# A macaron transformer block on one core: the stores of the scaled attention outputs issued by GpSimd in place of SyncE

## The chip, the cores and the metric

The kernel runs on 1 core of one Trainium2 chip. The metric is the device time of one execution in microseconds (us). Of the kernel before, three runs are shown, and one more execution was taken with the hardware profiler.

## The reference, cut to what matters

The input is x, of 2 batches of 1024 rows and 1024 columns (f32). Three residual layers follow one another: half an FFN with a LoRA branch, an attention layer, and the same half FFN again.

```python
x = x + 0.5 * ffn(layernorm(x), ...)
x = x + attn(layernorm(x), ...)
x = x + 0.5 * ffn(layernorm(x), ...)
# attn, H = 32 heads, causal, latent keys and values of 64 columns
q = rmsnorm(x @ wq_a.T, q_a_ln_w) @ wq_b.T            # then rope on 64 of 128 columns
kv = rmsnorm(ckv, kv_a_ln_w) @ wkv_b.T
scores = einsum("bqhd,bkhd->bhqk", q_full, k_full) * softmax_scale
attn = softmax(where(causal, scores, min))
out = einsum("bhqk,bkhd->bqhd", attn, v).reshape(B, S, H * VD) @ wo.T
```

The division by the row sums of the softmax is put off: the kernel multiplies the product of probabilities and values by the reciprocal row sums afterwards. This multiplication and the store of its result are what the change is about.

## The kernel before, in words

`macaron_block` (L1320) runs six phases one after another: constants, the first FFN, latents, attention, output projection, the second FFN. Each phase is a block with one instruction stream per engine, and the streams are tied together by semaphores alone. In every phase all DMAs are issued by SyncE (SP); GpSimd (POOL) issues none.

**The attention phase** has 32 steps: 16 pairs of heads times 2 batches. A step handles 1024 queries of two heads. What an engine does in a step, and in which order, is written out by hand in one table per engine (L697 to L705). An entry such as `P0-1` is job P, number 0, belonging to the step before; `A0+1` belongs to the step after. `rounds` (L754) runs the tables: a first round, a loop over rounds of two steps, a last round. The jobs that matter here:

- PE: `Q` (L923) projects queries, `S` (L940) scores, `V` (L957) probabilities times values, `F` (L913) and `W` (L966) fold weights. After V of one step come S8, S9 of the next and then Q0, with F0 and F1 between them in every second step.
- ACT: `Q` copies the projected queries out of PSUM in three instructions (L1004 to L1006), `H` (L1013) makes their high part, `E` (L1021) are the exponentials, `O` (L1036) evicts half of the values.
- DVE: `M` (L1071) masks and takes maxima, `T` (L1081) transposes, `R` (L1090, L1094) prepares the reciprocal row sums, `O` (`join_values`, L1106) adds up the values into `o_raw`. Before it overwrites `o_raw` it waits for the store of the step before (`o_stored`).
- POOL: `A` (`rotate`, L1136, L1138, L1140) is rope on 64 partitions in three instructions, `B` (`query_lo`, L1145) the low part of the queries, `P` (`scale_values`, L1152) multiplies `o_raw` by `o_scale` and counts up the semaphore `scaled`. Before each job POOL waits until the job before has ended (`finished`, L1156). Its order in a step is B2 B3, A0 A1 B0 B1 of the next step, P0 P1 of the step before, A2 A3 of the next step.
- SP: `X` (`turn_scales`, L861, L865) brings the reciprocal row sums through DRAM into `o_scale`, `Y` (`store_o`, L871) waits for `scaled` and stores 128 x 512 f32 (256 KB) of `o_raw` to `oT`, `K` and `L` load weights, `Z` (L876) stores a folded weight. SP takes them strictly in the order of its table, so Y0 and Y1 stand in front of K, L, X0 and Z. After the rounds SP waits for the last stores (L895) before the block can end.

`o_raw` and `o_scale` are parts of the tile `pT`, and the trace names both by that.

The scores of rows from 512 on (S8 to S15) need the queries of B2 and B3: `scores` waits for `q_lo` (L932). A2 to B3 of POOL therefore stand between P1 and S8 of PE.

The output projection (`output_phase`) loads `oT` (L1209) and the folded weights (L1215) with SP as soon as the attention block has ended.

Of the kernel before, what the change touches and what calls it, by code (L numbers as in the profile page):

```python
# [16 lines left out]
P = 128  # L17
BANK = 512
B, S, D = 2, 1024, 1024
# [16 lines left out]
CHUNK = 512  # L36
# [43 lines left out]
def later(n, least):  # L80

    return not isinstance(n, int) or n >= least
# [619 lines left out]
            "T6+0 R0+0 T7+0 O0-1 M8+0 O1-1 F0+0 M9+0 O2-1 T8+0 F1+0 M10+0 M11+0 T9+0 O3-1 M12+0 M13+0 T10+0 T11+0 "  # L702
            "M14+0")
POOL_STEP = ("B2+0 B3+0 A0+1 A1+1 B0+1 B1+1 P0-1 P1-1 A2+1 A3+1")
SP_STEP = ("X1-1 Y0-1 Y1-1 K0+0 L0+0 X0+0 Z0+0")  # L705


def parse(table):
# [45 lines left out]
def rounds(eng, body):  # L754
    body(Round(0, first=True))
    with eng.Fori(1, PAIRS - 1) as it:
        body(Round(it))
    body(Round(PAIRS - 1, last=True))


def attention_phase(nc, k, args, oT_d, rinv_d, wvo_d, v_d):
# [6 lines left out]
    with ExitStack() as stack:  # L768
# [20 lines left out]
        valued, copied, evicted, scaled = c.sem("valued"), c.sem("copied"), c.sem("evicted"), c.sem("scaled")  # L789
        o_stored = [c.sem(f"o_stored{ch}") for ch in range(2)]  # L790
# [6 lines left out]
        def spare(e, t0, t1):  # L797

            return pT[:, e, t0:t1, CHUNK:S]

        qf, swapped = spare(0, 0, 2), spare(0, 2, 4)
        o_raw, o_scale = spare(1, 0, 2), spare(1, 2, 4)
# [19 lines left out]
        def folds(it, n, s):  # L822

            return 2 * (it + (s + 1) // 2) + n + 1
# [9 lines left out]
        @block.sync  # L834
        def _(sp):
            def load_fold(pair):
                sp.dma_start(wn[:], wn_d[bass.ds(pair, 1), :, :].rearrange("a p n -> (a p) n").rearrange("p (e n) -> p e n", e=2)).then_inc(wn_in, 16)
                sp.dma_start(wpe[:].rearrange("p e r n -> p (e r n)"), wpe_d[bass.ds(pair, 1), :, :].rearrange("a p n -> (a p) n")).then_inc(wn_in, 16)

            def load_out(pair):  # L840
                sp.dma_start(wv[:].rearrange("p e n -> p (e n)"), wv_d[bass.ds(pair, 1), :, :].rearrange("a p n -> (a p) n")).then_inc(wo_in, 16)
                sp.dma_start(wo[:].rearrange("p e n -> p (e n)"), wo_d[bass.ds(pair, 1), :, :].rearrange("a p n -> (a p) n")).then_inc(wo_in, 16)

            load_out(0)
            for j in range(2):
                sp.wait_ge(k.v_stored[j], 8 * NT)
            for b in range(B):
                for i in range(BLOCKS):
                    rows = v_d[b * S:(b + 1) * S, :].rearrange("(m a c) v -> c a m v", a=BLOCKS, c=32)
                    for a in range(BLOCKS):  # L850
                        sp.dma_start(val[32 * i:32 * i + 32, b, a, :, :], rows[:, a, :, :]).then_inc(v_in[b], 16)

            def turn_scales(it, ch, s):

                step, x = it * 2 + s, 2 * QT * (s % 2) + QT * ch
                rows = rinv_d[bass.ds(step, 1), ch * S:(ch + 1) * S].rearrange("a (c q) -> (a c) q", q=P)
                sp.wait_ge(r_turned, step * 2 + ch + 1)
                for g in range(BLOCKS):
                    if g == BLOCKS - 1 and later(step, 1):
                        sp.wait_ge(scaled, step * 2 + ch - 1)  # L860
                    sp.dma_start(rows[:, 32 * g:32 * g + 32], rinvT[32 * g + x:32 * g + x + QT, x // QT, :]).then_inc(r_stored, 16)  # L861
                sp.wait_ge(r_stored, step * 128 + ch * 64 + 64)
                for e in range(2):
                    x = ch * S + e * CHUNK
                    sp.dma_start(o_scale[KVR * e:KVR * e + KVR, ch, :],  # L865
                                 rinv_d[bass.ds(step, 1), x:x + CHUNK].to_broadcast([KVR, CHUNK])).then_inc(r_loaded[ch], 16)

            def store_o(it, ch, s):
                b, pair = s % 2, it + s // 2
                sp.wait_ge(scaled, (it * 2 + s) * 2 + ch + 1)  # L870
                sp.dma_start(oT_d[bass.ds(pair * P, P), b * S + ch * CHUNK:b * S + (ch + 1) * CHUNK], o_raw[:, ch, :]).then_inc(o_stored[ch], 16)  # L871

            def store_w(it, s):
                half, pair = s % 2, it + s // 2
                sp.wait_ge(w_copied, it * 2 + s + 1)
                sp.dma_start(wvo_d[bass.ds(pair * P, P), half * BANK:(half + 1) * BANK],  # L876
                             wvo[:]).then_inc(w_stored, 16)

            def body(r):
                for job, n, s in r.jobs(SP_STEP):  # L880
                    if job == "X":
                        turn_scales(r.it, n, s)
                    elif job == "Y":
                        store_o(r.it, n, s)
                    elif job == "Z":
                        store_w(r.it, s)
                    elif job == "L":
                        sp.wait_ge(f_split, folds(r.it, 1, s - 1))
                        load_fold(r.it + s // 2 + 1)
                    elif job == "K":  # L890
                        sp.wait_ge(w_copied, r.it * 2 + s + 1)
                        load_out(r.it + (s + 1) // 2)
            rounds(sp, body)
            for ch in range(2):
                sp.wait_ge(o_stored[ch], 16 * 2 * PAIRS)  # L895
            sp.wait_ge(w_stored, 16 * 2 * PAIRS)
# [231 lines left out]
        @block.gpsimd  # L1128
        def _(pool):
            def rotate(it, n, s):  # L1130

                ch, number = n // 2, (it * 2 + s) * 4 + n
                x = slice(ch * CHUNK, (ch + 1) * CHUNK)
                plain, crossed = qf[64:128, n % 2, :], swapped[64:128, n % 2, :]
                pool.wait_ge(q_copied, number + 1)
                nc.gpsimd.tensor_tensor(plain, plain, cosT[64:128, x], ALU.mult).then_inc(rope_parts, 1)  # L1136
                pool.wait_ge(rope_parts, number * 2 + 1)
                nc.gpsimd.tensor_tensor(crossed, crossed, sinT[64:128, x], ALU.mult).then_inc(rope_parts, 1)  # L1138
                pool.wait_ge(rope_parts, number * 2 + 2)
                nc.gpsimd.tensor_tensor(plain, plain, crossed, ALU.add).then_inc(roped, 1)  # L1140

            def query_lo(it, n, s):
                x = slice(n // 2 * CHUNK, (n // 2 + 1) * CHUNK)
                pool.wait_ge(q_hi, (it * 2 + s) * 4 + n + 1)
                nc.gpsimd.tensor_tensor(q[:, n % 2, LO, x], qf[:, n % 2, :], q[:, n % 2, HI, x].bitcast(F32), ALU.subtract).then_inc(q_lo, 1)  # L1145

            def scale_values(it, ch, s):

                step = it * 2 + s
                pool.wait_ge(evicted, step * 4 + 4)  # L1150
                pool.wait_ge(r_loaded[ch], step * 32 + 32)
                nc.gpsimd.tensor_tensor(o_raw[:, ch, :], o_raw[:, ch, :], o_scale[:, ch, :], ALU.mult).then_inc(scaled, 1)  # L1152

            pool.wait_ge(tab_in, 48)

            def finished(it, job, n, s):  # L1156
                if job == "P":
                    pool.wait_ge(scaled, (it * 2 + s) * 2 + n + 1)
                else:
                    pool.wait_ge(roped if job == "A" else q_lo, (it * 2 + s) * 4 + n + 1)  # L1160

            def body(r):
                job, n, s = list(Round(0).jobs(POOL_STEP))[-1]
                before = None if r.first else (job, n, s - 2)
                for job, n, s in r.jobs(POOL_STEP):
                    if before:
                        finished(r.it, *before)
                    before = job, n, s
                    if job == "A":
                        rotate(r.it, n, s)  # L1170
                    elif job == "B":
                        query_lo(r.it, n, s)
                    elif job == "P":
                        scale_values(r.it, n, s)
            rounds(pool, body)
# [246 lines left out]
```

## Time and profile before

| | us |
|---|---|
| median of 3 runs | 1962.72 |
| lowest and highest | 1962.16, 1965.12 |
| the profiled execution, own time | 1964.07 |
| its span, first to last instruction | 1962.1 |
| granted TensorE clock, mean | 0.974 of full |

Busy time in the span: PE 1819.1 (93%), the weight loads of PE 1423.7, DVE 1230.6, ACT 997.6, POOL 870.1 (44%). The profiled execution is 1.35 us above the median. Its own time is 1.97 us above its span. Where a row says `x2` after two instructions that follow one another closely, its duration is that of both together. `[4.62 <-ACT pT L1006]` behind a row says that the engine stood idle for 4.62 us before it and what released it.

### The profile page before, as it was taken

What the parts mean: (1) busy time and instruction counts of PE and PEld (TensorE: products, weight loads), DVE (VectorE), ACT (ScalarE), POOL (GpSimd) and SP (SyncE); (2) the same over time, 40 slices, a digit from 0 to 9 for tenths busy, and PEclk for the clock granted to TensorE, in tenths of its full rate; (3) what the DMA queues carried; (4) which work ended last, traced back from release to release, by engine and by line L of the source; (5) the groups of instructions that cost most, each with busy time, mean ns of one, the idle gap of its engine ahead of it and who ended that gap; (6) DMA issues with size and microseconds to landing.
All of it is one profiled execution on the core that took longest, in us unless ns stands there. A gap on an engine that the chain in (4) does not pass through costs nothing. (4 is left out here: it accounts for less than half of the span.)

```text
span 1962.1 us, 44377 instructions
## 1 busy us (share of the span) xinstructions
PE 1819.1 (93%) x15472; PEld 1423.7 (73%) x15472; DVE 1230.6 (63%) x2653; ACT 997.6 (51%) x2135; POOL 870.1 (44%) x641
## 2 busy tenths in 40 slices
PE   6999968689999999999999999997699999979999
PEld 4678767667777777777777777775488888857887
DVE  5555356378889889888898888887421121125553
ACT  2211055478888888888887888885410010012110
POOL 2231110268777787787877877873000000004311
PEclk9999989899999999999999999999799999989999
DMA  6442152402221221211212212211742223224321
GB/s 224 167 167 91 60 150 71 107 23 70 65 77 50 71 77 55 83 60 55 83 60 72 66 49 83 66 67 56 261 134 88 86 96 117 65 107 158 132 86 65
DMA packets 111695, 182.45 MB, mean 93 GB/s; under 512 B 27472, under 2 KB 64464, under 8 KB 109584
## 3 DMA queue, kind: packets, MB, share of 16 engines
q1 hardware_dynamic: 111632, 181.61, 28.5%
q8 instruction: 39, 0.64, 0.1%
q14 instruction: 24, 0.20, 0.0%
HBM read 122.06 MB, written 59.51 MB: 93 GB/s over the span
## 5 line engine op out<-in xcount | busy, mean ns | idle before, releaser
L940 PE MATMUL psS<-keyT,q 128*128 128x512 f32 (+2 forms) x2304 | 474.3, 351 | 32.7 <-POOL q L1145 25.3
L940 PEld LDWEIGHTS psS<-keyT,q 128*128 128x128 f32 x2304 | 381.9, 190 | 127.6 <-DVE negmax L1071 41.4
L1021 ACT ACTIVATE prob<-prob,negmax 128x640 f32<-128x640 f32 (+7 forms) x512 | 391.9, 767 | 78.7 <-DVE negmax L1071 76.4
L1081 DVE STREAM_TRANSPOSE pT<-prob 128x640 f32<-128x640 f32 (+7 forms) x512 | 380.2, 762 | 66.3 <-PE psV L957 63.3
L1071 DVE CUSTOM_DVE_ANT_0 prob<-psS,mask 128x640 f32<-128x640 f32 (+7 forms) x512 | 371.9, 742 | 40.0 <-PE psS L940 26.3
L413 PE MATMUL f_psy<-f_weff,f_xT 128*128 128x512 f32 x1344 | 313.9, 393 | 0.0
L1307 PE MATMUL o_psy<-o_w,o_o 128*128 128x512 f32 x1344 | 304.8, 389 | 0.0
L1136 POOL TENSOR_TENSOR pT<-pT,cosT 64x512 f32<-64x512 f32 x128 | 164.6, 1286 | 302.6 <-ACT pT L1006 288.5
L1307 PEld LDWEIGHTS o_psy<-o_w,o_o 128*128 128x128 f32 x1344 | 252.3, 188 | 52.3
L413 PEld LDWEIGHTS f_psy<-f_weff,f_xT 128*128 128x128 f32 x1344 | 250.8, 188 | 54.0 <-issue 1.7
L957 PE MATMUL psV<-pT,val 32*64 32x512 f32 (+3 forms) x8192 | 264.8, 407 | 6.6 <-DVE pT L1081 6.2
L957 PEld LDWEIGHTS psV<-pT,val 32*64 32x64 f32 x8192 | 168.0, 132 | 110.7 <-issue 67.4
L245 POOL TENSOR_TENSOR f_weff<-f_w_in,f_weff 128x1024 fp32r<-128x1024 f32 x16 | 38.7, 2416 | 450.9 <-ACT f_weff L341 450.9
L923 PE MATMUL psV<-qnT,wq 128*128 128x512 f32 x768 | 195.4, 398 | 0.4 <-DVE wq L1062 0.4
L1281 DVE TENSOR_TENSOR o_y<-o_psy,o_x_in 128x512 f32<-128x512 f32 x32 | 22.0, 692 | 261.0 <-PE o_psy L1307 246.3
L312 POOL TENSOR_TENSOR f_xo<-f_xt,f_bias_half 128x1024 f32<-128x1024 f32 x32 | 80.4, 2512 | 219.6 <-DMA out<-f_xo 101.1
L1145 POOL TENSOR_TENSOR q<-pT,q 128x512 fp32r<-128x512 f32 x128 | 165.2, 1290 | 11.5 <-POOL pT L1140 2.2
L1240 ACT ACTIVATE o_o<-o_in 128x1024 fp32r<-128x1024 f32 x32 | 32.5, 1053 | 269.9 <-PE o_psy L1307 234.7
L1138 POOL TENSOR_TENSOR pT<-pT,sinT 64x512 f32<-64x512 f32 x128 | 165.1, 1290 | 10.1
L1140 POOL TENSOR_TENSOR pT<-pT 64x512 f32<-64x512 f32 x128 | 164.6, 1286 | 10.0
L923 PEld LDWEIGHTS psV<-qnT,wq 128*128 128x128 f32 x768 | 142.1, 191 | 28.6 <-DVE wq L1062 0.6
L163 ACT ACTIVATE f_xT<-f_ps_xT 128x512 fp32r<-128x512 f32 x64 | 34.9, 595 | 178.7 <-PE f_ps_xT L154 178.7
(99 smaller groups left out, 1882.3 us busy)
## 6 DMA issues: line engine op xcount, KB each, us to landing
wo<-in_wo SPq DMA_DIRECT2D x16, 1024.0 KB, 5.6
pT<-row_scales SPq DMA_DIRECT2D x128, 128.0 KB, 2.8
oT<-pT SPq DMA_DIRECT2D x64, 256.0 KB, 2.4
o_in<-oT SPq DMA_DIRECT2D x32, 512.0 KB, 5.2
f_xt<-in_x SPq DMA_DIRECT2D x16, 512.0 KB, 4.1
f_w_in<-in_w SPq DMA_DIRECT2D x16, 512.0 KB, 6.9
w_sum<-f_w_in SPq DMA_DIRECT2D x16, 512.0 KB, 5.1
x<-f_xo SPq DMA_DIRECT2D x16, 512.0 KB, 3.0
```

Of the source, the lines that this page charges most:

```text
L413: ins = nc.tensor.matmul(psy[:, j, half, :], f.xT[:, j, a, dt, :], weff[:, b, m, dt, half * BANK:(half + 1) * BANK], start=(i == 0 and dt ...
L923: ins = nc.tensor.matmul(psV[:, n, :], wq[:, a, e, t, :], k.qnT[:, m, t, b * S + ch * CHUNK:b * S + (ch + 1) * CHUNK], start=(i == 0 and t ...
L940: ins = nc.tensor.matmul(psS[:, slot, start + x0:start + x1], q[:, e, a, t * P:(t + 1) * P], k.keyT[:, m, b * S + x0:b * S + x1], start=(i ...
L957: ins = nc.tensor.matmul(out[:, :, kt:QT, :], val[rows, b, block, kt, :], pT[rows, :, kt:QT, x:x + 32], start=(kt == 0 and a == 0), stop=( ...
L1021: nc.scalar.activation(row, row, ACT.Exp, bias=negmax[:, n % 8:n % 8 + 1], scale=-1.0, accum_out=rowsum[:, column(n, s):column(n, s) + 1]) ...
L1071: nc.vector.tensor_tensor_reduce(out=prob[:, n % RING, 0:width], in0=place(n), in1=k.mask[:, S - width:S], scale=-1.0, scalar=LARGEST, op0 ...
L1081: nc.vector.transpose(pT[:, n % 2, t, 0:width], prob[:, n % RING, 0:width]).then_inc(turned, 1)
L1136: nc.gpsimd.tensor_tensor(plain, plain, cosT[64:128, x], ALU.mult).then_inc(rope_parts, 1)
L1138: nc.gpsimd.tensor_tensor(crossed, crossed, sinT[64:128, x], ALU.mult).then_inc(rope_parts, 1)
L1140: nc.gpsimd.tensor_tensor(plain, plain, crossed, ALU.add).then_inc(roped, 1)
L1145: nc.gpsimd.tensor_tensor(q[:, n % 2, LO, x], qf[:, n % 2, :], q[:, n % 2, HI, x].bitcast(F32), ALU.subtract).then_inc(q_lo, 1)
L1307: ins = nc.tensor.matmul(psy[:, j, half, :], o[:, j, a, pair, :], w[:, m, pair, half * BANK:(half + 1) * BANK], start=(pair == 0 and i == ...
```

## The change

SP no longer stores `o_raw`. In its place POOL, right behind each multiplication of `scale_values`, waits until that has ended and issues the same DMA itself, with the same semaphore for its completion. The order of the other jobs is unchanged.

```diff
-SP_STEP = ("X1-1 Y0-1 Y1-1 K0+0 L0+0 X0+0 Z0+0")
+SP_STEP = ("X1-1 K0+0 L0+0 X0+0 Z0+0")
...
-            def store_o(it, ch, s):
-                b, pair = s % 2, it + s // 2
-                sp.wait_ge(scaled, (it * 2 + s) * 2 + ch + 1)
-                sp.dma_start(oT_d[bass.ds(pair * P, P), b * S + ch * CHUNK:b * S + (ch + 1) * CHUNK], o_raw[:, ch, :]).then_inc(o_stored[ch], 16)
...
-                    elif job == "Y":
-                        store_o(r.it, n, s)
...
                 nc.gpsimd.tensor_tensor(o_raw[:, ch, :], o_raw[:, ch, :], o_scale[:, ch, :], ALU.mult).then_inc(scaled, 1)
+                b, pair = s % 2, it + s // 2
+                pool.wait_ge(scaled, step * 2 + ch + 1)
+                nc.gpsimd.dma_start(oT_d[bass.ds(pair * P, P), b * S + ch * CHUNK:b * S + (ch + 1) * CHUNK], o_raw[:, ch, :]).then_inc(o_stored[ch], 16)
```

## Rows read from the trace of the kernel before

**Rows 1.** Two steps: length, busy PE, PEld, DVE, ACT, POOL, PEclk, DMA share, GB/s.

```profile
554.05:614.51 60.46, 58.94 (x720) 44.10 (x721) 52.85 (x124) 50.17 (x111) 46.37 (x36) 1.00 0.20 67
```

**Rows 2.** Timeline of POOL, one step: start, us, line, what, idle before.

```profile
825.62 2.65 POOL L1145 TENSOR_TENSOR q<-pT,q 128x512 fp32r<-128x512 f32 x2 [0.16 <-POOL pT L1140]
832.90 1.30 POOL L1136 TENSOR_TENSOR pT<-pT,cosT 64x512 f32<-64x512 f32 x1 [4.62 <-ACT pT L1006]
...
844.15 2.66 POOL L1152 TENSOR_TENSOR pT<-pT 128x512 f32<-128x512 f32 x2 [0.26 <-POOL q L1145]
...
855.21 2.64 POOL L1145 TENSOR_TENSOR q<-pT,q 128x512 fp32r<-128x512 f32 x2
```

**Rows 3.** Timeline of PE: S8 and S9 behind V; first, two neighbouring and last.

```profile
493.54 1.13 PE L940 MATMUL psS<-keyT,q 128*128 128x384 f32 x6 [0.28 <-POOL q L1145]
...
827.05 1.11 PE L940 MATMUL psS<-keyT,q 128*128 128x384 f32 x6 [0.36 <-POOL q L1145]
828.42 1.11 PE L940 MATMUL psS<-keyT,q 128*128 128x384 f32 x6 [0.26 <-POOL q L1145]
829.37 1.53 PE L923 MATMUL psV<-qnT,wq 128*128 128x512 f32 x6
...
856.54 1.16 PE L940 MATMUL psS<-keyT,q 128*128 128x384 f32 x6 [0.35 <-POOL q L1145]
857.91 0.65 PE L913 MATMUL psV<-wn 64*128 64x64 f32 x4 [0.21 <-DVE pT L1106]
...
1310.97 1.11 PE L940 MATMUL psS<-keyT,q 128*128 128x384 f32 x6 [0.17 <-POOL q L1145]
```

**Rows 4.** Timeline of ACT: the copy of Q0 out of PSUM.

```profile
831.01 0.60 ACT L1004 ACTIVATE pT<-psV 128x512 f32<-128x512 f32 x1 [0.76 <-PE psV L923]
```

**Rows 5.** Waits, 451 to 1328 us: who waited for whom, us, times, longest.

```profile
POOL pT L1136 <- ACT pT L1006: 153.3, 29, 6.2
...
PE psS L940 <- POOL q L1145: 13.3, 42, 0.4
...
POOL pT L1152 <- POOL q L1145: 6.0, 28, 0.3
```

**Rows 6.** Waits of SP's queue, whole run.

```profile
SPq L871 <- POOL pT L1152: 540.3, 64, 21.8
```

**Rows 7.** Instructions on oT: count, duration ns min/median/max, first and last start.

```profile
L871 SPq DMA_DIRECT2D oT<-pT x64: 348/362/373, 452.7 to 1376.6; - x64
```

**Rows 8.** DMA issues: out<-in, count, KB each, median us to landing.

```profile
oT<-pT SPq DMA_DIRECT2D x64, 256.0 KB, 2.4
```

**Rows 9.** Timelines at the first and last of the 30 affected steps.

```profile
462.42 2.63 POOL L1145 TENSOR_TENSOR q<-pT,q 128x512 fp32r<-128x512 f32 x2 [0.16 <-POOL pT L1140]
...
464.17 2.15 PE L940 MATMUL psS<-keyT,q 128*128 128x384 f32 x12
...
1338.72 2.64 POOL L1145 TENSOR_TENSOR q<-pT,q 128x512 fp32r<-128x512 f32 x2
...
1340.32 2.31 PE L940 MATMUL psS<-keyT,q 128*128 128x384 f32 x12
```

**Rows 10.** Timeline at the end of the attention phase.

```profile
1373.97 2.60 POOL L1152 TENSOR_TENSOR pT<-pT 128x512 f32<-128x512 f32 x2 [21.86 <-DVE pT L1106]
1375.26 1.70 SPq L871 DMA_DIRECT2D oT<-pT  x2
1379.51 1.02 SPq L1209 DMA_DIRECT2D o_in<-oT  x2
```

**Rows 11.** Start of the output projection: a PE pause, then stretches (columns of rows 1).

```profile
1400.11 39.97 PE L1295 MATMUL o_psy<-o_w,o_o 128*128 128x512 f32 x168 [2.87 <-DVE o_w L1267]
...
1400.00:1402.00 2.00, 1.89 (x6) 1.55 (x7) 2.00 (x2) 2.00 (x3) 0.00 (x0) 0.68 0.70 182
1402.00:1404.00 2.00, 2.00 (x7) 1.51 (x6) 2.00 (x3) 0.90 (x2) 0.00 (x0) 0.50 0.68 215
1404.00:1406.00 2.00, 2.00 (x10) 1.65 (x9) 1.73 (x2) 0.66 (x1) 0.00 (x0) 0.97 0.96 322
```

## The prediction, made before the changed kernel ran

> **What bounds the kernel now.** I read the stretches first. In the attention phase two steps take 60.46 us, in which PE is busy 58.94, DVE 52.85, ACT 50.17 and POOL 46.37 [rows 1]. PE looks like the bound and POOL like an engine with 14 us to spare. The waits say otherwise: between 451 and 1328 us PE waits for the low part of the queries 42 times, 13.3 us in all, while POOL's own idle time ends with a copy by ACT, 29 times, 153.3 us [rows 5]. Those two waits belong to one loop, which the timelines show.
>
> Take POOL from its idle time on: A0 starts at 832.90; A0 A1 B0 B1, then P0 P1 at 844.15, then A2 A3, then B2 at 855.21 [rows 2]. B2 is the first half of a 2.64 us pair, so it ends at 855.21 + 1.3 = 856.5, and PE's S8 starts at 856.54, released by it [rows 3]. The way back stands one step earlier: B3 ends at 825.62 + 2.65 = 828.27 [rows 2]; S9 starts at 828.42 and Q0 follows at 829.37 for 1.53 us [rows 3]; ACT begins to copy Q0 at 831.01, three instructions of 0.6 us [rows 4], to 832.8; A0 starts at 832.90 [rows 2]. No link has slack: POOL to PE to ACT to POOL. The 4.62 us (5.97 in every other step) that POOL stands idle are the time that PE and ACT need for their part of the loop, not room for more work. Whatever is put between A0 and B2 lengthens the step by its full time. S8 waits for POOL like this in 28 steps on end, from 493.54 to 1310.97 us [rows 3].
>
> **What is removed.** SP issues 64 stores at 0.36 us each [rows 7], 23 us of its queue, and stands 540.3 us in front of them waiting for POOL [rows 6]. This frees K, L and X0, which stand behind Y1 in SP's table, up to 20 us earlier. I cost the gain at nothing: in the steady stretch what POOL's P0 waits for is POOL itself [rows 5], not the row scales that SP brings, and no wait of PE is for a weight load. The scales of X0 still can't land before P0 of the step before has read the old ones.
>
> **What is added.** Two DMA issues on POOL per step, each behind its P. Each wait for `scaled` is for a multiplication whose end POOL waits for before its next job anyway; I cost the waits at nothing beyond the issue. Queued behind DMA 0 is P1; behind DMA 1 are A2, A3, B2, B3, and for B2 waits S8 of PE. So both issues lie in the loop.
>
> The price c of one issue on POOL is not in the trace, since no DMA is issued there. From below it is bounded by SP's issue of the same DMA, 0.36 us [rows 7]. From above I take POOL's own period for a whole 128 x 512 multiplication: P0 and P1 together take 2.66 and one takes 1.30, so 1.36 us [rows 2]. I take 1.0, nearer the upper end: what POOL does it does as an instruction of its own kind, with a hand-over of 0.16 us in front of it where it had to wait [rows 2], and a list of 128 rows is to be made. The Trainium skill (DMA: Bandwidth & Descriptors, "Latency and other measured facts") states about 1 us until the first byte of a DMA of GpSimd against 0.6 from SP, the difference being descriptors written by its own cores; if all of that 1 us held POOL, an estimate by that page would be the same sum as mine.
>
> **The sum**, against the profiled execution (1964.07 us, 1.35 above the median of the runs):
> - 30 steps have P0 and P1 ahead of A2 (those of steps 0 to 29; the last two P pairs come after the last B): 30 x 2 x 1.0 = +60.0.
> - Cover: in the first of them B2 ends at 462.42 + 1.31 = 463.73 and S8 starts at 464.17, so 0.44 is free; in the last 1338.72 + 1.32 = 1340.04 against 1340.32, 0.28 [rows 9]. In every other step F0 waits 0.21 for DVE behind S8 [rows 3]; 14 x 0.21 = 2.9. Together -3.6.
> - The end of the phase is on the path: the block closes when the last store has landed. DMA 0 delays P1 by 1.0, and the last store is given out 1.0 instead of 0.36 after P1's end. +1.6. The transfer itself, 2.4 us to landing [rows 8], is unchanged. Today the multiplications end at 1376.57 and the next load is issued at 1379.51 [rows 10].
> - DVE waits for the store before it overwrites `o_raw`. The store would land some 2.6 us later than today, and DVE has a whole step before it needs the tile: `o_stored` of a step is asked for behind the next step's V, which ends just before S8, some 9 us after P1 (844.15 + 2.66 = 846.81 to 856.54 [rows 2, 3]), against 2.6 + 2.4 us [rows 8]. Nothing.
> - POOL's P31 pair has 21.86 us of idle time before it [rows 10], so P30 costs nothing.
>
> 60.0 - 3.6 + 1.6 = +58.0. That is 2022.1 for the profiled execution and 1962.72 + 58.0 = 2020.7 against the median; I forecast 2020. With c = 0.36: 21.6 - 3.6 + 0.4 = +18.4, so 1981. With c = 1.36: 81.6 - 3.6 + 2.4 = +80.4, so 2043.
>
> **Rivals.**
> *The second issue is hidden.* P uses 128 partitions, A only 64 (the other half of the tile), yet both take 1.30 us [rows 2]: time follows the length, so half of POOL idles in A. If the part of POOL that makes the DMA isn't needed by A2, DMA 1 runs beside it, and only DMA 0 and a hand-over of about 0.1 are left: 30 x 1.1 = 33.0, - 3.6 + 1.6 = +31.0, 1993.7. The Trainium skill (GPSIMD Engine Reference, "2.1 Instruction dispatch") has this rule: each of POOL's cores goes on to the next instruction when its own share is done. Against it stands that nothing here shows two POOL instructions side by side; in this trace POOL waits for the end of each. Chance 0.17.
>
> *The clock falls.* The longer step shows as a PE pause before S8: 0.35 + 2c, plus 0.25 before S9. In the output projection a PE pause of 2.87 us was followed by a fall of the granted clock from 1.00 to 0.50, and PE ran 13 matmuls in 4 us where it runs 10 in 2 us at full clock: 7 fewer at 0.2 us, 1.4 us lost [rows 11]. With c = 1.0 the pause is 2.35 and stays under that. From c = 1.26 on it is as long. Then c = 1.3 gives 78.0 - 3.6 + 2.2 = +76.6, and with a fall in every third step 10 x 1.4 = +14 more: 2053; in every step +42, 2081. For it speaks that S8, S9 and Q0, which the fall would hit, are links of the loop. Chance 0.08.
>
> *Not slower.* If POOL only hands the transfer over, as SP's engine does in 0.36 us with others waiting for nothing, and spends far less than that, the two hand-overs vanish in the 3.6 us of cover. It decides from c below 0.13 us on: 60c - 3.6 + 2c - 0.36 is then under 3.9 us, which is 0.2% and about what a measurement of this kernel can tell from no change. At c = 0.05 it is -0.9 us: 1962. A true gain would need someone who waits for what SP can now issue earlier, and I found nobody. Chance 0.10, of it 0.02 for faster.
>
> *The issue costs POOL more than one of its multiplications* (c above 1.36, clock unchanged): each 0.1 adds 6.2 us. Chance 0.05.
>
> **Numbers.** The forecast, both issues paid, c between 0.36 and 1.36, has 0.60, and its own range is 1981 to 2043. The hidden second issue (0.17) lies inside it. To have 8 in 10 I take the upper end to 2055, which holds the fall of the clock in every third step and c up to 1.55. Left out are the not-slower case and the two upper tails. Slower by over 0.2%: 0.90; within: 0.08; faster: 0.02.
>
> **What would show it.** 64 DMA issues on POOL, none of `oT` on SP; two steps of 60.46 us grown to about 64.3; POOL's idle time before A0 unchanged at 4.6 and 6.0 us, since it is the other engines' part of the loop; PE's wait for POOL before S8 grown from 0.35 to about 2.35; between P0 and P1, and between P1 and A2, gaps of about 1 us each (a gap only before P1: the hidden issue); the granted clock still 1.00; SP's 540 us wait moved to other lines. I am wrong if the idle time before A0 shrinks by what the issues take: then it was slack after all. I am wrong in the price if the gaps are far from 1.0, and each 0.1 us of it is worth 6 us.

## The result and the profile after

The changed kernel takes 2081.86 us (median of 4 runs, 2079.43 to 2084.94) against 1962.65 for the kernel before: a ratio of 1.060, 95% interval 1.059 to 1.062. It is slower, as forecast, but by 119 us in place of 58, and outside the range (1981 to 2055). The span of the profiled execution grew from 1962.1 to 2081.7 us, by 119.6.

From the page of the changed kernel: busy time by engine; two DMA queues (packets, MB, share of 16 engines); the group that grew most (busy, mean ns, idle before it and its releaser); the moved DMA (KB each, us to landing).

```profile
PE 1871.4 (90%) x15472; PEld 1473.0 (71%) x15472; DVE 1232.3 (59%) x2653; ACT 992.8 (48%) x2135; POOL 906.7 (44%) x705
...
q1 hardware_dynamic: 102416, 164.83, 24.5%
q0 software_dynamic: 5120, 16.78, 2.1%
...
L933 PE MATMUL psS<-keyT,q 128*128 128x512 f32 (+2 forms) x2304 | 499.2, 366 | 97.9 <-POOL q L1138 89.1
...
oT<-pT POOLq DMA_DIRECT2D x64, 256.0 KB, 3.2
```

The 64 stores have left SP's queue for a software queue, and POOL has 641 + 64 = 705 instructions. PE's wait for POOL in front of the scores has become 89.1 us of idle time (25.3 in the kernel before). PE itself is busy 52 us longer (1871.4 against 1819.1) with the same 15472 matmuls: that is no wait, that is a slower clock.

POOL's timeline in the changed kernel, one step, to be laid beside [rows 2] (L1129 opens A, L1145 is P, L1148 the store, L1138 is B):

```profile
815.08 1.29 POOL L1129 TENSOR_TENSOR pT<-pT,cosT 64x512 f32<-64x512 f32 x1 [5.66 <-ACT pT L999]
...
826.33 1.29 POOL L1145 TENSOR_TENSOR pT<-pT 128x512 f32<-128x512 f32 x1 [0.26 <-POOL q L1138]
828.31 0.58 POOL L1148 DMA_DIRECT2D oT<-pT  x1 [0.69 <-POOL pT L1145]
828.91 1.31 POOL L1145 TENSOR_TENSOR pT<-pT 128x512 f32<-128x512 f32 x1
830.87 0.58 POOL L1148 DMA_DIRECT2D oT<-pT  x1 [0.65 <-POOL pT L1145]
831.53 1.27 POOL L1129 TENSOR_TENSOR pT<-pT,cosT 64x512 f32<-64x512 f32 x1
...
839.81 2.63 POOL L1138 TENSOR_TENSOR q<-pT,q 128x512 fp32r<-128x512 f32 x2
851.11 1.30 POOL L1129 TENSOR_TENSOR pT<-pT,cosT 64x512 f32<-64x512 f32 x1 [8.67 <-ACT pT L999]
```

An issue costs POOL 0.58 us and, ahead of it, 0.65 to 0.69 us in which it does nothing that is recorded: from P0 to P1 there are 2.58 us where there were 1.36, so 1.22 per issue. From A0 to the end of B3 there are 839.81 + 2.63 - 815.08 = 27.36 us, where it was 855.21 + 2.64 - 832.90 = 24.95 [rows 2]: 2.41 more per step. And the idle time in front of A0, which I had expected unchanged, is 8.67 us in one step (5.97 before) and 5.66 in the other (4.62 before). So something in the part of the loop that belongs to PE and ACT has become longer too. PE's timeline and the stretches of the same step show it (the stretches have the columns of [rows 1]):

```profile
841.13 1.15 PE L933 MATMUL psS<-keyT,q 128*128 128x384 f32 x6 [2.76 <-POOL q L1138]
...
843.25 1.97 PE L933 MATMUL psS<-keyT,q 128*128 128x384 f32 x6
...
846.19 2.93 PE L916 MATMUL psV<-qnT,wq 128*128 128x512 f32 x6
...
840.00:842.00 2.00, 0.87 (x6) 0.87 (x6) 0.83 (x2) 2.00 (x5) 1.92 (x2) 1.00 0.00 0
842.00:844.00 2.00, 2.00 (x9) 1.75 (x8) 1.49 (x4) 0.80 (x3) 0.44 (x1) 0.56 0.00 0
...
846.00:848.00 2.00, 2.00 (x6) 1.56 (x6) 1.32 (x5) 1.28 (x4) 0.00 (x0) 0.50 0.00 0
```

A PE pause of 2.76 us before S8; then the granted clock falls from 1.00 to 0.50, from 2.4 to 1.2 GHz, and S9 takes 1.97 us in place of 1.1, Q0 2.93 in place of 1.53. Read in short stretches over the attention phase, the clock falls behind 24 of the 30 lengthened pauses and stays down for 3 to 7 us each time, 130 us in all; in the same steps of the kernel before (451 to 1340 us) it never falls. The falls hit the very matmuls through which the loop runs.

**The theory** after this: two terms. 30 steps x 2.41 us of POOL, 72 us; and some 42 us from the clock. **Rivals:** (A) the issues and their software queue cost all of it, and the clock is a bystander that changes nothing, since PE waits for POOL anyway; (B) SP's new order brings data late.

### The profile page after: what moved, and what is told of

It reads as the page before. It is cut to its first block and busy times, and to the rows that moved or that the text cites. A ratio compares the mean times of both kernels' runs of the same rounds, so it can differ in the third digit from the quotient of the medians.

```text
span 2081.7 us, 44365 instructions
## 1 busy us (share of the span) xinstructions
PE 1871.4 (90%) x15472; PEld 1473.0 (71%) x15472; DVE 1232.3 (59%) x2653; ACT 992.8 (48%) x2135; POOL 906.7 (44%) x705
## 5 line engine op out<-in xcount | busy, mean ns | idle before, releaser
L933 PE MATMUL psS<-keyT,q 128*128 128x512 f32 (+2 forms) x2304 | 499.2, 366 | 97.9 <-POOL q L1138 89.1
L933 PEld LDWEIGHTS psS<-keyT,q 128*128 128x128 f32 x2304 | 409.0, 203 | 192.8 <-issue 50.7
L1129 POOL TENSOR_TENSOR pT<-pT,cosT 64x512 f32<-64x512 f32 x128 | 164.2, 1283 | 346.5 <-ACT pT L999 333.5
L916 PE MATMUL psV<-qnT,wq 128*128 128x512 f32 x768 | 214.5, 426 | 0.4 <-DVE wq L1055 0.4
L916 PEld LDWEIGHTS psV<-qnT,wq 128*128 128x128 f32 x768 | 154.6, 208 | 32.5 <-DVE wq L1055 0.6
L1138 POOL TENSOR_TENSOR q<-pT,q 128x512 fp32r<-128x512 f32 x128 | 164.7, 1287 | 11.4 <-POOL pT L1133 2.2
L1006 ACT ACTIVATE q<-pT 128x512 fp32r<-128x512 f32 x128 | 80.2, 627 | 84.9 <-POOL pT L1133 82.4
```

The source lines that it names most:

```text
L916: ins = nc.tensor.matmul(psV[:, n, :], wq[:, a, e, t, :], k.qnT[:, m, t, b * S + ch * CHUNK:b * S + (ch + 1) * CHUNK], start=(i == 0 and t ...
L933: ins = nc.tensor.matmul(psS[:, slot, start + x0:start + x1], q[:, e, a, t * P:(t + 1) * P], k.keyT[:, m, b * S + x0:b * S + x1], start=(i ...
```

## Experiments: is it the clock, the issue or SP?

**One: keep PE busy in the pause.** The changed kernel, with extra matmuls in front of S8:

```diff
+                if n == 8:
+                    for _ in range(12):
+                        nc.tensor.matmul(psS[:, 0, P:BANK], k.keyT[:, HI, b * S:b * S + P], k.keyT[:, HI, b * S:b * S + BANK - P],
+                                         start=True, stop=True)
                 if t % 4 == 0:
                     pe.wait_ge(q_lo, step * 4 + t // 4 * 2 + e + 1)
```

> The changed kernel with 12 more matmuls of 384 columns on PE ahead of S8 in every step (they write the place in PSUM that S8 is about to fill; the result is not touched), some 2.2 us of work in a PE pause of 2.3 to 2.8 us. Theory (two terms: 1.22 us of POOL per issue in the loop, and a fall of the clock that the longer pause brings): the clock stays at 1.00 in the attention phase, POOL's idle time before A0 goes back to 4.6 and 6.0 us, and the time falls from 2082 to about 1963 + 30 x 2.44 - 3.6 + 2 = 2035 (2030 to 2045). Rival A (the whole loss is the issue on POOL and what comes with it, the clock is a bystander): the clock comes back and the time stays at 2075 or above. Rival B (SP's new order makes data late): no change either.

Measured: 2043.53 us, ratio 1.039 (1.036 to 1.042). 384 added matmuls (12 in each of 32 steps) make the kernel 42 us faster than the changed one (1.060 - 1.039 = 0.021 of 1964). Timelines of this kernel, PE, then POOL:

```profile
825.99 2.35 PE L926 MATMUL psS<-keyT 128*128 128x384 f32 x12 [0.15 <-issue]
828.65 1.16 PE L937 MATMUL psS<-keyT,q 128*128 128x384 f32 x6 [0.32 <-POOL q L1142]
...
802.54 1.30 POOL L1133 TENSOR_TENSOR pT<-pT,cosT 64x512 f32<-64x512 f32 x1 [4.65 <-ACT pT L1003]
...
835.92 1.29 POOL L1133 TENSOR_TENSOR pT<-pT,cosT 64x512 f32<-64x512 f32 x1 [5.96 <-ACT pT L1003]
```

The extra work lies in what was the pause, S8 follows at full clock, no fall is left in these steps, and POOL's idle times are those of the kernel before to 0.03 us. Rival A falls for these 42 us. Two steps now take 65.28 us (731.30 to 796.58) against 60.46: 2 x 2.41, the POOL term alone.

**Two: the same time on POOL without any DMA.** The kernel before, with a second, shorter multiplication per scaling. The first 432 of 512 columns of `o_raw` are scaled twice.

```diff
+                nc.gpsimd.tensor_tensor(o_raw[:, ch, 0:432], o_raw[:, ch, 0:432], o_scale[:, ch, 0:432], ALU.mult).then_inc(dummied, 1)
+                pool.wait_ge(dummied, step * 2 + ch + 1)
                 nc.gpsimd.tensor_tensor(o_raw[:, ch, :], o_raw[:, ch, :], o_scale[:, ch, :], ALU.mult).then_inc(scaled, 1)
```

> The kernel before, all stores by SP, with a second multiplication of 128 x 432 ahead of each scaling on POOL, some 1.1 us and a hand-over of 0.14: about the time of an issue. (The first 432 columns of o_raw are scaled twice.) No DMA is issued by POOL. Theory (it is only time on POOL, wherever it comes from): as the changed kernel, 2070 to 2090, with the same falls of the clock. Rival A in the form that the software queue itself costs (descriptors, transfers, contention): clearly less, 2035 or under. Rival B (SP's order): back to 1963 to 2035, since SP's order is the old one.

Measured: 2084.07 us, ratio 1.060 (1.054 to 1.066), with 21 falls of the clock and 119 us of half clock in the same steps. Its POOL timeline:

```profile
825.37 1.12 POOL L1153 TENSOR_TENSOR pT<-pT 128x432 f32<-128x432 f32 x1 [0.26 <-POOL q L1146]
826.57 1.29 POOL L1155 TENSOR_TENSOR pT<-pT 128x512 f32<-128x512 f32 x1
827.94 1.13 POOL L1153 TENSOR_TENSOR pT<-pT 128x432 f32<-128x432 f32 x1
829.15 1.28 POOL L1155 TENSOR_TENSOR pT<-pT 128x512 f32<-128x512 f32 x1
```

With SP's old order, with the old queue for every store and with 1.2 us of arithmetic per store, the loss is the same within the intervals, which are some 12 us wide to either side. The two terms need neither the software queue nor SP's new order: rival B falls. It is time on POOL in this place. What an interval of 12 us would hide is the few us that POOL's own stores cost at the end of the phase; they are read there from the timeline.

**Three: one of the two stores.** POOL issues only the second, SP has Y0 back.

```diff
-SP_STEP = ("X1-1 K0+0 L0+0 X0+0 Z0+0")
+SP_STEP = ("X1-1 Y0-1 K0+0 L0+0 X0+0 Z0+0")
...
+                if ch == 0:
+                    return
                 b, pair = s % 2, it + s // 2
                 pool.wait_ge(scaled, step * 2 + ch + 1)
                 nc.gpsimd.dma_start(oT_d[bass.ds(pair * P, P), b * S + ch * CHUNK:b * S + (ch + 1) * CHUNK], o_raw[:, ch, :]).then_inc(o_stored[ch], 16)
```

> Only the second of the two stores of a step is issued by POOL, the first by SP as before. Theory: one issue lengthens POOL's part of the loop by 1.22 us, the pause before S8 is about 1.6 us and the clock stays at 1.00: 30 x 1.22 - 3.6 + 1 = +34, so 1997 (1990 to 2003). Rival A, all of the loss is per issue (119/2 = 60 each): 2022. The hidden second issue of the prediction: under 1970.

Measured: 2008.19 us, ratio 1.021 (1.017 to 1.025). That is 42 us lost where I had expected 34 and at most 40: the clock did not hold throughout. It fell 5 times, 17 us in all, behind 5 of 28 pauses of 1.46 to 1.59 us. Still, one issue costs 42 us and two cost 119; the loss is not proportional, because the longer pause brings more and longer falls.

**Four: both issues behind both multiplications**, P0 P1 DMA0 DMA1:

```diff
-POOL_STEP = ("B2+0 B3+0 A0+1 A1+1 B0+1 B1+1 P0-1 P1-1 A2+1 A3+1")
+POOL_STEP = ("B2+0 B3+0 A0+1 A1+1 B0+1 B1+1 P0-1 P1-1 Y0-1 Y1-1 A2+1 A3+1")
```

> Both stores issued by POOL behind both multiplications: P0 P1 DMA0 DMA1 A2. Theory: of the 1.22 us of an issue 0.58 is the DMA instruction and 0.65 the time from the end of the multiplication to it (hand-over and address registers); for DMA0 this 0.65 now lies beside P1, so the issues cost about 1.8 us per step in place of 2.44. The pause before S8 is about 2.1 us. If the clock holds: 1963 + 54 - 3.6 + 2 = 2015; if it still falls as often, 2060. If the 0.65 isn't hidden by P1, no change, 2080.

Measured: 2009.88 us, ratio 1.022 (1.019 to 1.025): 72 us better than the changed kernel (75 by the ratios) with the same instructions. Its POOL timeline:

```profile
831.15 2.67 POOL L1145 TENSOR_TENSOR pT<-pT 128x512 f32<-128x512 f32 x2 [0.17 <-POOL q L1138]
833.76 1.25 POOL L1150 DMA_DIRECT2D oT<-pT  x2
835.08 1.27 POOL L1129 TENSOR_TENSOR pT<-pT,cosT 64x512 f32<-64x512 f32 x1
```

Both recordless times in front of the issues are gone, not one of two as I expected. From P0 to A2 there are 3.93 us (831.15 to 835.08), where the kernel before has 2.82 (844.15 to 846.97) and the changed kernel 5.20 (826.33 to 831.53): 1.11 for two issues in place of 2.38. So the instruction costs 0.56 to 0.58 and the way to it 0.65, and the latter costs nothing where POOL has something to do meanwhile. What it is made of I did not take apart, but at the end of the phase, where the addresses are constants, it is 0.30 us, which points to the addresses that are worked out from the loop's register for about half of it. The pause before S8 is 1.4 to 1.6 us here in the steady steps, and the clock still fell 4 times, 17 us. One such fall, stretches of this kernel around a pause of 1.43 us that ended at 1035.51:

```profile
1034.00:1036.00 2.00, 0.57 (x11) 0.52 (x4) 0.86 (x3) 2.00 (x5) 1.82 (x2) 1.00 0.62 166
1036.00:1038.00 2.00, 1.74 (x10) 1.57 (x9) 1.15 (x3) 0.74 (x3) 0.73 (x1) 0.79 0.00 0
1038.00:1040.00 2.00, 2.00 (x7) 1.70 (x7) 1.61 (x6) 0.72 (x2) 0.00 (x0) 0.50 0.00 0
```

**Five: the same with PE filled** (7 matmuls, 1.3 us, in front of S8).

> The kernel with both issues behind both multiplications, plus 7 matmuls of 384 columns on PE ahead of S8 (some 1.3 us in a pause of 1.6). Theory: its 4 falls of the clock go and with them about 10 us: 1963 + 30 x 1.15 - 3.6 + 2 = 1996 (1994 to 2003 with what the shorter steps leave). If the falls were harmless: 2008 to 2012.

Measured: 2002.69 us, ratio 1.019 (1.017 to 1.021). No fall is left, and by the ratios it is some 5 us faster, with intervals that overlap; the sign is as expected, the size not settled. Two steps take 62.75 us (529.09 to 591.84), where two steps without a fall took 62.74 in the kernel without the filling (529.71 to 592.45), so the filling itself costs nothing. Without any cover the sum is 30 x 1.145 = 34.4 us, and the end of the phase adds 3.7 (from the end of P1, 1410.77, to the next load, 1417.39, there are 6.62 us against 2.94): together the measured 38.

**Six: does an issue run beside an instruction of half the partitions?** Both issues inside A2, whose instructions use partitions 64 to 127:

```diff
                 nc.gpsimd.tensor_tensor(plain, plain, cosT[64:128, x], ALU.mult).then_inc(rope_parts, 1)
+                if pending:
+                    store_o(*pending.pop(0))
                 pool.wait_ge(rope_parts, number * 2 + 1)
                 nc.gpsimd.tensor_tensor(crossed, crossed, sinT[64:128, x], ALU.mult).then_inc(rope_parts, 1)
+                if pending:
+                    store_o(*pending.pop(0))
```

> Both stores issued by POOL inside A2, behind its first and its second instruction, which use partitions 64 to 127 only. Theory: the 0.65 us of preparation is hidden as it was with the issues behind both multiplications, the 0.58 us of the issue is not: 1.1 to 1.3 us per step, 2005 to 2015 as that one. The rival of the prediction (a POOL instruction of half the partitions runs beside the making of the DMA): the step stays within 0.3 us of the kernel before, 1963 to 1975.

Measured: 2014.90 us, ratio 1.026 (1.023 to 1.028). The timeline of POOL:

```profile
839.58 1.30 POOL L1131 TENSOR_TENSOR pT<-pT,cosT 64x512 f32<-64x512 f32 x1 [0.16 <-POOL pT L1151]
840.82 0.58 POOL L1156 DMA_DIRECT2D oT<-pT  x1
841.42 1.29 POOL L1135 TENSOR_TENSOR pT<-pT,sinT 64x512 f32<-64x512 f32 x1
842.65 0.58 POOL L1156 DMA_DIRECT2D oT<-pT  x1
...
844.70 1.28 POOL L1131 TENSOR_TENSOR pT<-pT,cosT 64x512 f32<-64x512 f32 x1 [0.16 <-POOL pT L1139]
```

An issue starts 0.06 us before its neighbour is recorded as ended and then holds the next one up. A2 takes 844.70 - 839.58 = 5.12 us where it took 4.17 (846.97 to 851.14 in the kernel before): 0.47 per issue. The instructions stand one behind the other, although those of A2 leave partitions 0 to 63 alone. The clock fell 8 times (48 us of half clock), behind pauses of 1.29 to 1.40 us. That fits that this kernel is no better than the one with 1.11 us per step: a microsecond of half clock cost 41.3 / 130 = 0.32 us in the changed kernel, and by this estimate 31 us more of it cost 10 us, against the 30 x 0.17 = 5 us that are saved.

**Seven: put the issues into POOL's idle time**, behind B3 of the step after:

```diff
-POOL_STEP = ("B2+0 B3+0 A0+1 A1+1 B0+1 B1+1 P0-1 P1-1 A2+1 A3+1")
+POOL_STEP = ("B2+0 B3+0 Y0-2 Y1-2 A0+1 A1+1 B0+1 B1+1 P0-1 P1-1 A2+1 A3+1")
```

> Both stores issued by POOL in its idle time, behind B3 of the step after. Theory: nothing is added to the part of POOL that S8 waits for, but the store of a step now lands some 5 us after DVE wants to overwrite o_raw (O0 starts at 827.4 in the trace of before, B3 ends at 828.3, issue 1.3 and landing 3.2 us behind it): DVE stands 5 us in front of O0, and with it M8 and the rest: 2060 to 2130, with PE pauses that bring falls of the clock. If POOL's idle time were free for this: 1963 to 1970.

Measured in a single run: 2154.51 us, 190 above the kernel before. DVE's timeline and its wait:

```profile
834.64 0.85 DVE L1099 TENSOR_TENSOR pT<-psV,cosT 64x256 f32<-64x256 f32 x2 [4.53 <-DMA oT<-pT]
...
DVE pT L1099 <- DMA oT<-pT: 141.5, 29, 5.5
```

DVE stands 4.9 us per step (141.5 / 29) before it may overwrite `o_raw`, PE waits for DVE, and the clock falls in every step (198 us at half clock). POOL's idle time is there, but it comes just when DVE wants the tile back.

## Experiments: is the loop through POOL really what sets the step?

If it is, the kernel before can be made faster by taking something out of it. The second multiplication of a step moves to DVE (with a semaphore of its own for each half), all stores stay with SP. First behind O3:

```diff
-"T8+0 F1+0 M10+0 M11+0 T9+0 O3-1 M12+0 M13+0 T10+0 T11+0 "
+"T8+0 F1+0 M10+0 M11+0 T9+0 O3-1 P1-1 M12+0 M13+0 T10+0 T11+0 "
...
-POOL_STEP = ("B2+0 B3+0 A0+1 A1+1 B0+1 B1+1 P0-1 P1-1 A2+1 A3+1")
+POOL_STEP = ("B2+0 B3+0 A0+1 A1+1 B0+1 B1+1 P0-1 A2+1 A3+1")
```

> The kernel before (all stores by SP), with the second multiplication of a step moved from POOL to DVE, behind O3. If the loop through POOL sets the step, taking 1.36 us out of it gives back what PE waits in front of S8 and S9: 0.6 us in one step, 0.35 in the next, then PE itself is the bound: 30 x 0.48 = -14, so 1949 (1945 to 1955). If DVE's 0.7 us more per step (and its sharing of a port with POOL) is on the path instead, 1963 to 1985.

Measured: 1988.66 us, ratio 1.012 (1.010 to 1.013): slower. Waits between 451 and 1340 us in this kernel:

```profile
PEld psS L940 <- DVE negmax L1071: 79.8, 97, 1.6
...
PE psS L940 <- DVE negmax L1071: 35.7, 56, 0.7
```

PE no longer waits for POOL, but for DVE's maxima, which now come 0.7 us later in a place where PE asks for them at once. So I moved it to the place where DVE stands idle for 1.5 us, in front of T0:

```diff
+"M15-1 T12-1 T13-1 M0+0 T14-1 M1+0 M2+0 M3+0 T15-1 M4+0 M5+0 P1-2 T0+0 ..."
```

> The kernel before with the second multiplication of a step on DVE again, but now in front of T0, where DVE stands idle 1.5 us in every step waiting for the first of V. Theory (the loop through POOL sets the step; the try behind O3 failed because it pushed DVE's maxima, for which PE then waited): the 0.7 us fit into DVE's idle time, POOL's part of the loop is 1.36 us shorter and PE no longer waits in front of S8 and S9: 1945 to 1957. If DVE is the bound everywhere as soon as anything is added to it: 1975 or above. If the loop through POOL is not what sets the step of the kernel before: 1961 to 1966.

Measured: 1956.80 us over 6 runs against 1963.08 over 10, ratio 0.9966 (0.9954 to 0.9978): faster than the kernel before by 6 us, and so than both. Timelines of this kernel, DVE, then PE, then POOL:

```profile
817.85 0.69 DVE L1113 TENSOR_TENSOR pT<-pT 128x512 f32<-128x512 f32 x1
819.40 0.31 DVE L1081 STREAM_TRANSPOSE pT<-prob 128x128 f32<-128x128 f32 x1 [0.86 <-PE psV L957]
...
825.46 1.16 PE L940 MATMUL psS<-keyT,q 128*128 128x384 f32 x6
826.77 1.12 PE L940 MATMUL psS<-keyT,q 128*128 128x384 f32 x6 [0.16 <-POOL q L1153]
...
856.32 0.65 PE L913 MATMUL psV<-wn 64*128 64x64 f32 x4 [0.37 <-DVE pT L1106]
...
818.02 1.66 POOL L1148 TENSOR_TENSOR pT<-pT 64x512 f32<-64x512 f32 x1
```

The multiplication fits into the idle time, and S8 no longer waits for POOL. The 1.36 us less do not all arrive: the instruction of POOL that runs beside DVE's multiplication takes 1.66 us here (1.78 in the step after) in place of 1.29, A2 waits 0.4 to 0.6 us for ACT, and from A0 to the end of B3 there are 24.32 us (831.27 to 855.59) against 24.95. Of the 0.63 us the step gains only about 0.2, since PE, and DVE in front of F0, are now the next bound. The loop sets the step of the kernel before, but with little room beneath it.

## Why the prediction was right and wrong

**The loop: right.** Time put between A0 and B2 came back in full. With PE filled, two steps grew by 4.82 us, and POOL's part from A0 to the end of B3 had grown by 2.41 in one. The idle time before A0 is not slack; the seventh experiment shows what happens to one who takes it for that.

**SP's relief: right** within the intervals, nothing came of it; the second experiment loses the same with SP's old order. The Trainium skill says the like (DMA: Bandwidth & Descriptors, "Issuing engines are not separate DMA queues"): another issuer saves only the time that the sequencer takes to issue. Here the side that saved it had nobody waiting, and the side that got it had.

**The price of an issue: close.** 1.22 us against 1.0, within my bounds (0.36 and 1.36). The term 30 x 2 x 1.0 = 60.0 measures 30 x 2.41 = 72.3. More than half of an issue lies in what I had costed at nothing beyond it, the way from the end of the multiplication: 0.65 us, against 0.58 for the issue itself.

**The cover of 3.6 us: not there.** I let a 0.21 us wait of F0 swallow a part of the delay. With PE filled that wait is still there, now in front of F1, because the DVE work it waits for stands behind M8, and M8 behind S8.

**The end of the phase: too small.** I had +1.6. The timeline of the changed kernel there:

```profile
1487.92 1.25 POOL L1145 TENSOR_TENSOR pT<-pT 128x512 f32<-128x512 f32 x1 [20.17 <-DVE pT L1099]
...
1490.07 1.27 POOL L1145 TENSOR_TENSOR pT<-pT 128x512 f32<-128x512 f32 x1
1491.63 0.58 POOL L1148 DMA_DIRECT2D oT<-pT  x1 [0.30 <-POOL pT L1145]
1497.78 1.04 SPq L1205 DMA_DIRECT2D o_in<-oT  x2
```

P1 starts 2.15 us behind P0, not 1.3, so 0.85 later, and from its end (1491.34) to the next load of SP there are 6.44 us against 2.94 [rows 10]: +3.5. Together +4.3. What the block's end waits for stands at its own line, L768. The sequencers' instructions there (name, duration in ns, start), in the changed kernel, then in the kernel before:

```profile
L768 POOLq DRAIN  x1: 5910/5910/5910, 1491.6 to 1491.6; - x1
L768 SPq DRAIN  x1: 7/7/7, 1494.6 to 1494.6; - x1
...
L768 POOLq DRAIN  x1: 1364/1364/1364, 1375.3 to 1375.3; - x1
L768 SPq DRAIN  x1: 7/7/7, 1379.3 to 1379.3; - x1
```

SP has seen the last store land and is at the block's end at 1494.6. POOL's `DRAIN`, which ended 2.6 us ahead of that point in the kernel before (1376.7 against 1379.3), now lasts 5.91 us, to 1497.5, and the next phase starts right behind it. I had put only the delay of the last store into the sum; that the block closes behind POOL's own `DRAIN` too, and that this grows when POOL issues the stores, I had left out.

**The step that failed** is the one in the rival on the clock: "With c = 1.0 the pause is 2.35 and stays under that." I had one row with a fall, behind a pause of 2.87 us [rows 11], and used it as the shortest pause that brings one. One row bounds that only from above, and the trace of the kernel before has others that the prediction does not use. Two PE pauses in it, and the stretches around the second one (columns of [rows 1]):

```profile
21.80 1.97 PE L154 MATMUL f_ps_xT<-ident,f_xn 128*128 128x128 f32 x8 [2.62 <-DVE f_xn L144]
...
369.40 0.55 PE L638 MATMUL ps<-ident,lat 128*128 128x128 f32 x3 [2.20 <-DVE lat L672]
...
369.00:370.00 1.00, 0.55 (x3) 0.31 (x3) 0.88 (x5) 0.01 (x1) 0.00 (x0) 0.94 0.02 8
370.00:371.00 1.00, 0.00 (x0) 0.00 (x0) 0.43 (x2) 0.54 (x2) 0.00 (x0) 0.50 0.16 33
```

The clock fell at the end of the pause of 2.62 us (granted clock 0.68 from 21 to 23 us and 0.50 behind it), and again at about 369.9 us, behind the pause of 2.20 us and the 3 matmuls that follow it. So nothing put 2.35 us on a safe side. Eleven pauses of 1.1 to 1.3 us between 285 and 357 us brought no fall. In the changed kernel the pauses of 1.7 to 3.0 us brought 24 falls in 30 steps, those of about 1.5 us brought 5 and 4 in the kernels with one issue and with both behind the multiplications, and those of 1.3 to 1.4 us brought 8 with the issues inside A2. Nor does the length alone decide: in the changed kernel a pause of 1.90 us (ended at 534.25) brought a fall, and one of 2.64 (ended at 877.14) and four more of 2.57 to 2.64 brought none. The mechanism was written down, with its place and its price for a fall in every step (+42 us, 30 falls at 1.4); measured as the difference between the changed kernel and its filled copy it is 42 us, but from 24 falls at 1.7. That the 42 agree, and that the rival's 2081 is the measured time to 1 us, is partly luck: its terms were 78.0 - 3.6 + 2.2 for what measures 72.3 + 0 + 4.3. What was wrong is its chance, 0.08, and with it the upper end of the range. The sum that the runs give: 72.3 (POOL) + 41.3 (clock, 2081.7 - 2040.4 in spans) + 4.3 (end) = 117.9, of 119.6.

**The hidden second issue: wrong**, from P1 to A2 there are 2.62 us, much as from P0 to P1 (2.58). The Trainium skill's rule (GPSIMD Engine Reference, "2.1 Instruction dispatch"), that each core goes on by itself, did not help either: in the sixth experiment the issue overlapped its neighbours by some 0.1 us, no more.

**What I named as signs:** the 64 issues, the gaps (1.2 to 1.3 us, for about 1) and PE's pause of 2.35 (measured 1.9 to 3.0 but for the last) came; 64.3 us for two steps were 67.9 and 68.6, and the clock and the idle time before A0 did not stay.

## What to carry to other kernels

Before moving an instruction onto an engine with low busy time, follow the waits around once: if they close a loop through that engine, its idle time belongs to the others, and each microsecond put into its part of the loop counts once per step. A pause that such a move puts in front of PE has a second price, the clock, and it is paid in the links behind the pause; one row with a fall says that its pause is long enough, not that a shorter one is safe. Here pauses of 0.36 us brought none, of 1.3 to 1.6 us some and of 1.9 to 3.0 us most, so in this kernel the fall belongs into the sum with a weight from 1.3 us on. If GpSimd must issue a DMA, put the issue behind another instruction of its own that doesn't depend on it, not right behind the one that it waits for: here the same two issues cost 1.11 us so and 2.38 otherwise. And if it issues the last store of a phase, look at what its `DRAIN` adds to the phase's end.

## What the runs showed that I had not expected

- An issue on GpSimd is recorded with 0.58 us, but right behind the instruction that it waits for it costs 1.22. The rest is in no busy time, only in the idle column.
- Matmuls that compute nothing made a kernel 42 us faster, by keeping the clock at 2.4 GHz through the wait.
- After the last store of GpSimd, SP's next load comes 5.6 us after the issue has ended (1492.21 to 1497.78), and the stretches from 1494 to 1498 show no DMA traffic at all; after SP's store it comes 2.5 us after (1376.96 to 1379.51). The time is POOL's `DRAIN` at the block's end: 5.9 to 6.1 us in each kernel in which POOL issues both stores, 4.2 with one store (the load comes 3.8 us after the issue's end), 1.4 with the added multiplications and no store of POOL. What POOL does in that time, no run shows.
